# P and normalised x as fp16 planes turned by DMA, and scores, values and feed-forward of three query groups interleaved in 16 slots

## The reference

```python
def attn(x):                       # x already layer-normalised
    qkv = x[:, :, :64].fp16 @ w[:64].fp16 + x[:, :, 64:192] @ w[64:192] + x[:, :, 192:].fp16 @ w[192:].fp16
    q, k, v = split(qkv)
    s = softmax((q / sqrt(256)) @ k.T)
    return (s @ v) @ out_w.T + out_b

def ffn(x):                        # x already layer-normalised
    x_prev = x shifted by one token, zero ahead of the first
    r = sigmoid((mu_r * x + (1 - mu_r) * x_prev) @ W_r.T)
    k = relu((mu_k * x + (1 - mu_k) * x_prev) @ W_k.T) ** 2
    return r * (k @ W_v.T)

x = x + layernorm(attn(layernorm(x)))
x = x + layernorm(ffn(layernorm(x)))
```

## Time and profile before

| | |
|---|---|
| median of 3 runs | 1007.12 us (1006.1 to 1007.22) |
| span of the profiled execution, first to last instruction | 1005.9 us |
| PE busy | 969.4 us (96%) |
| DVE busy | 779.2 us (77%) |
| ACT busy | 555.6 us (55%) |
| POOL busy | 367.6 us (37%) |
| DMA queue of the kernel | 9.0% of 16 engines |
| mean granted TensorE clock | 0.991 of full |

### The profile page before, as it was taken

One profiled execution on the slowest core, in us unless ns is written; L12 is line 12 of the kernel. 1 busy time (PEld: TensorE's weight loads), 2 busy tenths in 40 slices (PEclk: granted clock), 3 DMA queues, 4 the chain that ended last, 5 costly groups with the idle time before them and its releaser, 6 DMA issues.

```text
span 1005.9 us, 16314 instructions
## 1 busy us (share of the span) xinstructions
PE 969.4 (96%) x5480; PEld 826.4 (82%) x5480; DVE 779.2 (77%) x1951; ACT 555.6 (55%) x936; POOL 367.6 (37%) x487
## 2 busy tenths in 40 slices
PE   5999999999999999999999999999999999999964
PEld 4788888888888888888888888888888888888953
DVE  5647678798877868888786867879887786877788
ACT  5744636475763736546674563647576463654533
POOL 2202434252542514434252342515344251443334
PEclk9999999999999999999999999999999999999987
DMA  6200000010100401010010400001000010101001
GB/s 183 65 20 22 1 22 22 1 43 1 42 2 14 113 3 43 1 42 2 1 43 1 126 1 24 23 1 43 1 31 13 0 43 1 43 1 34 10 1 42
DMA packets 44763, 28.28 MB, mean 28 GB/s; under 512 B 18432, under 2 KB 44416, under 8 KB 44672
## 3 DMA queue, kind: packets, MB, share of 16 engines
q1 hardware_dynamic: 44672, 27.14, 9.0%
HBM read 18.75 MB, written 8.39 MB: 27 GB/s over the span
## 4 chain that ended last, share of the span: by engine, by line
PE 92%; DVE 5%; ACT 1%; issue 1%; SPq 1%; DMA 0%; POOL 0%; POOLq 0%; DVEq 0%
PE S L1185 10%; PE S L1158 6%; PE S L1164 6%; PE S L1160 6%; PE S L1159 6%; PE S L1163 6%; PE M L1115 6%; PE M L1116 6%; PE M L1117 6%; PE Y L1314 6%; PE Y L1315 6%; PE Y L1319 6%; PE Y L1316 6%; PE Y L1318 5%; PE M L1206 1%; DVE att L819 1%
## 5 line engine op out<-in xcount | busy, mean ns | idle before, releaser
L728 DVE TENSOR_TENSOR pt_lo<-S,pt_hi 128x512 fp32r<-128x512 f32 x256 | 172.0, 676 | 114.7 <-ACT pt_hi L459 114.1
L774 DVE TENSOR_SCALAR_CACHE_REDUCE probs<-S 128x512 f32<-128x512 f32 x256 | 169.4, 682 | 72.4 <-PE S L1164 71.6
L459 ACT ACTIVATE pt_hi<-S 128x512 fp32r<-128x512 f32 x256 | 150.0, 596 | 80.2 <-PE S L1185 71.9
L504 ACT ACTIVATE probs<-probs,neg_max 128x2048 f32<-128x2048 f32 (+2 forms) x80 | 132.7, 1661 | 39.8 <-DVE scaled_max L778 39.8
L1185 PEld LDWEIGHTS S<-ident,probs 128*128 128x128 f32 x936 | 115.0, 141 | 27.5 <-DVE q_lo L728 0.4
L1185 PE MATMUL S<-ident,probs 128*128 128x128 f32 x936 | 135.9, 272 | 0.0
L1314 PE MATMUL Y<-pt_hi,v_hi 128*128 128x512 f32 x240 | 109.0, 454 | 0.3 <-ACT pt_hi L459 0.3
L837 DVE RECIPROCAL tmp<-tmp 128x256 f32<-128x256 f32 x60 | 104.6, 1743 | 0.0
L1158 PE MATMUL S<-xt_low,q_hi 128*128 128x512 f32 x256 | 102.2, 399 | 1.2 <-DVE wt_lo L728 0.5
L1164 PE MATMUL S<-xt_hi,q_lo 128*128 128x512 f32 x256 | 101.1, 395 | 0.0
L1160 PE MATMUL S<-xt_lo,q_hi 128*128 128x512 f32 x256 | 101.0, 395 | 0.0
(11 more groups left out here) (218 smaller groups left out, 2205.6 us busy)
## 6 DMA issues: line engine op xcount, KB each, us to landing
x_res<-in_L_attn_x SPq DMA_DIRECT2D x16, 512.0 KB, 3.3
out_x<-gate SPq DMA_DIRECT2D x15, 512.0 KB, 2.9
xin<-in_L_attn_x SPq DMA_DIRECT2D x32, 128.0 KB, 3.2
xin<-in_L_attn_x SPq DMA_DIRECT2D x16, 256.0 KB, 3.7
out_x<-gate SPq DMA_DIRECT2D x2, 256.0 KB, 2.1
probs<-in_L_attn_weight_qkv SPq DMA_DIRECT2D x3, 128.0 KB, 2.7
probs<-in_L_attn_weight_qkv SPq DMA_DIRECT2D x1, 256.0 KB, 3.0
tmp<-in_L_attn_out_w SPq DMA_DIRECT2D x1, 256.0 KB, 3.9
```

Of the source, the lines that this page charges most:

```text
L728: return dve.tensor_tensor(out_lo, psum, f32(hi), ALU.subtract)
L774: dve.tensor_scalar(probs[:, t, c * BLK:(c + 1) * BLK], S[u % 4][:, :], 1.0, None, ALU.mult, ALU.max, accum_out=chunk_max[:, t, c:c + 1]). ...
```

## The change

**What it does.** (1) Normalised x is scaled by 2^11 and written by ACT and DVE as three fp16 planes for each 128-token tile: columns 0 to 127, columns 128 to 255, and the remainder of the latter (`planes`). One DMA transpose for each 512-token block (`turn_planes`) makes `turned` from them. The planes serve as values, the turned planes as keys. (2) P is made as exp with a bias that scales it by 2^15, then split by ACT (`probs_high`) and DVE (`probs_low`) in two fp16 planes of 128x2048, and each plane is turned by one DMA transpose from SP (`turn_probs`): 8 a group, of 512 KB each. (3) The folded query-key weights and the queries become fp16 pairs too, scaled by a maximum found on the chip (`weight_scale`, `weight_factors`). (4) Scores and values are fp16 products: five of 512 columns for a unit as before, and five of 256 columns for each of 16 key tiles in each half of a group (`attend`), 160 in place of 80. (5) The stages are gone: in each of 16 slots of a step g, PE makes one score unit of group g and two key tiles of group g-1, and the projection, norms and feed-forward of group g-2 (its end reaches into g+1) lie in slots given by a table. There are 19 steps (`LAST`): the first has scores alone, the 17th has values but no scores, the last two only what follows. (6) Sigmoid is one ACT instruction; exp plus one and the reciprocals on DVE go. (7) The last group's work in halves goes. (8) Blocks of x are loaded to two buffers and prepared every tenth slot.

The core of the diff (setup of weights and unchanged feed-forward bodies left out):

```diff
+    PROJECT, ATTEND, NORM_ATT, RESIDUAL, RES_STATS, MIX_IN, TURN = 2, 3, 4, 5, 7, 8, 9
+    MIX, SPLIT_MIX, RECEPT, KEYS, SQUARE, VALUES, GATE, NORM_GATE, FINISH, STORE = 11, 12, 13, 14, 15, 17, 18, 19, 19, 21
+    QUERY = 6
+    LAST = 19
...
-        xt_low = sb("xt_low", [P, N], F32R)
-        xt_hi = sb("xt_hi", [P, N], F32R)
-        xt_lo = sb("xt_lo", [P, N], F32R)
-        v_hi = sb("v_hi", [P, NKT, D], F32R)
-        v_lo = sb("v_lo", [P, NKT, P], F32R)
+        planes = sb("planes", [P, 2, NKT, 3, P], F16)
+        turned = sb("turned", [P, 2, NKT, 3, P], F16)
...
+        probs = sb("probs", [P, 2, N])
+        p_hi = sb("p_hi", [P, 2, N], F16)
+        p_lo = sb("p_lo", [P, 2, N], F16)
+        pt_hi = sb("pt_hi", [P, 2, NKT, HALF], F16)
+        pt_lo = sb("pt_lo", [P, 2, NKT, HALF], F16)
...
+            def turn_planes(n):
+                b, i = divmod(n, NJ)
+                kts = slice(i * NT, (i + 1) * NT)
+                if b >= 2 and i == 0:
+                    sp.wait_ge(s_done, (b - 1) * NJ * UNITS)
+                sp.wait_ge(plane_lo_made, n + 1)
+                sp.dma_start_transpose(turned[:, b % 2, kts].rearrange("p k l t -> p (k l) t"),
+                                       planes[:, b % 2, kts].rearrange("p k l d -> p (k l d)")).then_inc(xt_in[i], 16)
+
+            def turn_probs(g, t):
+                a, cols = t // PT, slice((t % PT) * P, (t % PT + 1) * P)
+                if g >= 1:
+                    sp.wait_ge(pv_done, 2 * (g - 1) + a + 1)
+                sp.wait_ge(p_hi_made, g * NT + t + 1)
+                sp.dma_start_transpose(pt_hi[:, a, :, cols], p_hi[:, t % 2, :]).then_inc(pt_in[t], 16)
+                sp.wait_ge(p_lo_made, g * NT + t + 1)
+                sp.dma_start_transpose(pt_lo[:, a, :, cols], p_lo[:, t % 2, :]).then_inc(pt_in[t], 16)
...
+            for g in range(LAST):
+                for s in range(UNITS):
+                    if s == 1 and 1 <= g <= G:
+                        turn_probs(g - 1, 2)
+                    if s == 4 and 1 <= g <= G:
+                        turn_probs(g - 1, 3)
+                    if s == 8 and g < G:
+                        turn_probs(g, 0)
+                    if s == 11 and g < G:
+                        turn_probs(g, 1)
+                    if (n := prep(g, s, 6)) is not None:
+                        turn_planes(n)
+                    if (n := prep(g, s, -8)) is not None:
+                        reload_x(n)
+                    if (q := at(g, s, STORE)) is not None:
+                        store(q)
+                    if s == 9 and 1 <= g <= G:
+                        load_residual(g - 1)
...
+            def probs_high(g, t):
+                n = g * NT + t
+                act.wait_ge(exp_made, n + 1)
+                if n >= 2:
+                    act.wait_ge(pt_in[(t + 2) % NT], 32 * ((n - 2) // NT + 1))
+                copy(p_hi[:, t % 2, :], probs[:, t % 2, :]).then_inc(p_hi_made, 1)
...
+            def receptance(q):
+                for i in range(2):
+                    act.wait_ge(rec_done, q * 2 + i + 1)
+                    act.activation(rec[:, i, :], M[i][:, :], ACT.Sigmoid).then_inc(rec_made, 1)
...
+            def score_out(g, u):
+                t, c = unit(g, u)
+                n = g * UNITS + u
+                dve.wait_ge(s_done, n + 1)
+                if c == 0 and g * NT + t >= 2:
+                    dve.wait_ge(p_lo_made, g * NT + t - 1)
...
+            def probs_low(g, t):
+                dve.wait_ge(p_hi_made, g * NT + t + 1)
+                dve.tensor_tensor(p_lo[:, t % 2, :], probs[:, t % 2, :], p_hi[:, t % 2, :],
+                                  ALU.subtract).then_inc(p_lo_made, 1)
...
-            def turn_probs(g, kt):
-                if kt == 0:
-                    pe.wait_ge(exp_made, g * EXPS + NT)
-                if kt == NC:
-                    pe.wait_ge(exp_made, (g + 1) * EXPS)
-                for t in range(NT):
-                    mm = pe.transpose(T[kt % 4][:, t * P:(t + 1) * P], probs[:, t, kt * P:(kt + 1) * P], ident[:, :])
-                mm.then_inc(p_turned, 1)
...
+            def attend(g, a, kt):
+                b = g // NJ
+                if kt == 0:
+                    for t in range(a * PT, (a + 1) * PT):
+                        pe.wait_ge(pt_in[t], 32 * (g + 1))
...
+                pe.matmul(to[:, 0, :], low, p_h, start=first, stop=False, skip_group_check=True)
+                pe.matmul(to[:, 0, :], low, p_l, start=False, stop=final, skip_group_check=True)
+                pe.matmul(to[:, 1, :], high, p_h, start=False, stop=False, skip_group_check=True)
+                pe.matmul(to[:, 1, :], high, p_l, start=False, stop=False, skip_group_check=True)
+                mm = pe.matmul(to[:, 1, :], rest, p_h, start=False, stop=final, skip_group_check=True)
...
+            for g in range(LAST):
+                for s in range(UNITS):
+                    if g < G:
+                        scores(g, s)
+                    if 1 <= g <= G:
+                        attend(g - 1, s // 8, 2 * (s % 8))
+                        attend(g - 1, s // 8, 2 * (s % 8) + 1)
```

More of the change, by code:

```diff
@@ L122, in sandwich @@
         xm_lo = sb("xm_lo", [P, 2, HALVES, BLK], F32R)
-        yk_hi = sb("yk_hi", [P, HALVES, BLK], F32R)
-        yk_lo = sb("yk_lo", [P, HALVES, BLK], F32R)
+        rec = diff
         S = [bank(f"S{i}") for i in range(4)]
-        T = S[2:] + S[:2]
-        Y = [bank(f"Y{i}") for i in range(HALVES)]
+        Y = [bank(f"Y{i}") for i in range(2)]
         M = [bank(f"M{i}") for i in range(2)]
[L131 to L136, removed]
         def f32(ap):
@@ L537, in squares, with copy @@
[L537 to L549 removed]
+            def copy(out_, in_, scale=1.0):
+                return act.activation(out_, in_, ACT.Copy, scale=scale)
@@ L1133, in queries @@
-            def queries(j, banks):
-                tokens = bass.ds(j * BLK, BLK)
+            def queries(g):
+                b, j = divmod(g, NJ)
+                pe.wait_ge(xt_in[j], 16 * (b + 1))
+                kts = slice(j * NT, (j + 1) * NT)
+                low, high, rest = (turned[:, b % 2, kts, l, :] for l in range(3))
                 for m in range(HALVES):
                     cols = slice(m * P, (m + 1) * P)
-                    two(banks[m][:, :], wt_hi[:, QK, 0, cols], wt_lo[:, QK, 0, cols], xt_low[:, tokens], True, False)
-                    three(banks[m][:, :], wt_hi[:, QK, 1, cols], wt_lo[:, QK, 1, cols], xt_hi[:, tokens],
-                          xt_lo[:, tokens], False, True).then_inc(q_done, 1)
@@ new lines, in queries, with scores @@
+                    pe.matmul(to, qk_hi[:, 0, cols], low, start=True, stop=False)
+                    pe.matmul(to, qk_lo[:, 0, cols], low, start=False, stop=False)
+                    pe.matmul(to, qk_hi[:, 1, cols], high, start=False, stop=False)
+                    pe.matmul(to, qk_hi[:, 1, cols], rest, start=False, stop=False)
+                    pe.matmul(to, qk_lo[:, 1, cols], high, start=False, stop=True).then_inc(q_done, 1)
+            def scores(g, u):
+                t, c = unit(g, u)
+                n, b = g * UNITS + u, g // NJ
@@ new lines, in scores @@
+                if n >= 4:
+                    pe.wait_ge(s_copied, n - 3)
+                rows, kts = slice(t * P, (t + 1) * P), slice(c * NT, (c + 1) * NT)
+                low, high, rest = (turned[:, b % 2, kts, l, :] for l in range(3))
+                to = S[n % 4][:, :]
+                pe.matmul(to, q_hi[:, g % 2, 0, rows], low, start=True, stop=False)
+                pe.matmul(to, q_lo[:, g % 2, 0, rows], low, start=False, stop=False)
+                pe.matmul(to, q_hi[:, g % 2, 1, rows], high, start=False, stop=False)
```

1489 lines of the change are left out of this document (512 added, 977 removed).

## The result

The changed kernel takes 1093.44 us (median of 4 executions, 1088.53 to 1100.53) beside 1007.17 us for the kernel before. The ratio is 1.086, with a 95% interval of 1.082 to 1.090. The forecast was 891 us, faster. The profiled execution took 1090.8 us with a span of 1088.9.

What follows compares the result with a forecast made beforehand. PE's own work was taken to bound the kernel. 27 + 25 + 37 + 707 (14 steps of 49.5 + 1) + 37 + 57 gave 890 us of span, 891 measured; own range 854 to 953, for 8 in 10 up to 1130.

Steps and rivals of the forecast that it cites:

- PE's work: PE's products in one group: 49.5 us after the change, with 48.4 and 51.9 kept as ends; 59.93 before.
- The DMA term: Turned planes of P and x: 8.75 DMA transposes a group, 26 us of DMA in 50, beside PE.
- (b): DMA binds: PE waits for turned P in slots 0 and 8, T above 5.8 us, slower than before; chance 0.22.
- (c): DMA turns each plane 128x128 tile after tile with latency exposed, T 53 us, time 7 ms; chance 0.05.
- T: DMA engines' time for one transpose of 512 KB: taken as 3 us, between ends of 2.1 and 360.
- the sign given: In the profile after, a DMA transpose was to land in under 6 us.
- I charge 1 us of waits a step, and keep 0 and 3: PE's waits on late results in each steady step: 1 us, range 0 to 3, on top of 49.5.
- the 57 us a step: Stated sign of error: the prediction is wrong if a step exceeds 57 us for any reason.
- 15 of 19 us: Old group's chain from projection in slot 2 to the mixed input's turn in slot 9: needs 15 us of 19.
- the four score banks: PE runs four score banks ahead, three slots or 9 us, set against late results on other engines.
- rival (a): In-order waits: a late result each step, from POOL or DVE, costs 4 to 7 us; 933 to 975; chance 0.14.
- Start and tail: Outside the steady steps: 27 us to first scores, step 0 25, step 1 37, step 16 37, tail 57.

Runs made afterwards that it cites:

- the moves: Against the kernel after: DVE's gating ahead of the low plane, ACT's attention norm behind the high plane, ACT's sigmoid ahead of the high plane; 975.25 us, ratio 0.969.
- the fastest: DVE multiplies the gate ahead of slot 2's score unit, on top of the reordered tanh kernel with later chain and x blocks every 13th slot; 928.1 us, ratio 0.921.
- tanh: Sigmoid made as (1 + tanh(x/2))/2, on top of the kernel with three instruction moves; 967.71 us, ratio 0.961.
- spread out: Blocks of x prepared every 13th slot in place of every 10th, on top of the kernel with the old group's chain a slot later; 940.59 us, ratio 0.934.
- quarters: Each low plane of P made by DVE as four instructions of 512 columns, on top of the kernel with the old group's chain a slot later; 985.85 us, ratio 0.979.

## Why the prediction was wrong

**PE's work was right.** I took 49.5 us a group. Score products now stand 0.215 us apart and products of 256 columns 0.109 (timeline of the kernel after, the ends of a run of four intervals and of one of nine):

```profile
474.38 0.38 PE L806 MATMUL S<-turned,q_hi 128*128 128x512 f16 x1
...
475.24 0.38 PE L810 MATMUL S<-turned,q_lo 128*128 128x512 f16 x1
...
480.50 0.27 PE L825 MATMUL Y<-pt_hi,planes 128*128 128x256 f16 x1
...
481.48 0.27 PE L829 MATMUL Y<-pt_hi,planes 128*128 128x256 f16 x1
```

By the earlier trace rows they were 0.232 and 0.118. Scores 80 x 0.215 = 17.2, values 160 x 0.109 = 17.4, queries 2.2, the rest unchanged at 12.2: 49.0 us, near the good end of 48.4. The guess that most of the excess over 213 ns would go with fp16 fits. That reading 4-byte operands is its cause was not tested.

**The DMA term was right, and (b) and (c) fell.** T was put at 3 us. The queue's 41.6% of 16 engines is 7248 engine-us; less the traffic of before, 9.0% of its 16 x 1005.9 = 1448, and over 128 planes of P and 16 of x at three quarters, that is 2.6 us a plane, and the planes' packets come to some 20 ns each, as the 256- and 512-byte runs of the earlier trace rows had it at 22. Rival (b) needed 5.8. A transpose lands 3.8 to 4.0 us after its issue in the median, and never later than 5.9, where 6 was the sign given:

```profile
pt_hi<-p_hi SPq DMA_TRANSPOSE x64, 3.8
pt_lo<-p_lo SPq DMA_TRANSPOSE x64, 4.0
```

Of the Trainium skill's two figures, the 261 GB/s of DMA: Bandwidth & Descriptors, section on latency and other measured facts (by it T is an estimated 2.0 us), was the nearer. The 1309 ns a tile of VectorE: DVE Perf Modes, section on the three transpose paths, by which rival (c) had 2.9 ms, is not the rate here: 16 tiles of a plane cost 2.6 us.

**The step that failed** is "I charge 1 us of waits a step, and keep 0 and 3". The waits were 10.4 us a step, and PE's busy time was 4.4 us a step over the forecast, most of it slower clock behind the waits; that gives 64.3 by the window and 64.0 by the markers. It passed the 57 us a step beyond which the prediction called itself wrong. Three things went wrong in it.

First, it was priced from loads and not from queues. DVE at 80% and ACT at 73% of a 50 us step do leave room, and after the moves they fit: the same instructions ran at 55.3 us a step. But room says nothing about order. In the text I followed single results and asked only whether each had time in all ("15 of 19 us"); I did not set down, slot by slot, what stands ahead of each one on its engine. I named the low plane of 2.3 us, but behind the gating of slot 1, as the one that waits. It was the one that others wait behind, and so was ACT's high plane of 1.9.

Second, the slack I set against them was the four score banks. They cover a late evacuation of scores: PE waited for that 8.0 us in the whole kernel, all in step 0. They do not cover a product of the old group, which stands in PE's own order between score units. There one late bank stops everything.

Third, rival (a) had the mechanism, the places ("PE waits for DVE or POOL in slots 9 to 14") and even the table loads, but with a price of 4 to 7 us for one late result. There were four in each step, they add up, and the clock adds to them. The forecast with 13.5 us more in fourteen steps is 1080, close to what was measured. Its chance was 0.14; it should have been the forecast's equal. And for a case on the far side of 1007 I had looked to DMA alone.

**The clock** had no term at all. It stood at 0.62 behind a wait of 2.4 us and at 0.93 over four steps. Over the twelve steps between the markers PE's products were busy 643.4 us at 0.93 in the kernel after, and 603.0 us at 0.99 in the fastest, whose twelve steps take 619.2 us. So 40 of the 149 us between them, 3.4 a step, are busy time, the rest is idle time. No run changed the clock without changing the waits.

**Start and tail** were 19 and 17 us too short. The first scores came at 24.4 us, before the 27 I gave. Of the 19 us 9 are lost in step 0: first value product at 60.7 where I had 52, with the planes of the first tiles in series behind exp. The other 10 lie between it and the first marker, where the same waits of PE begin. The fastest kernel keeps 10 of the 19 and 12 of the 17: 12 x 1.1 + 10 + 12 is 35 of the 36 us by which its span of 926.1 stands over the forecast. So, once its order is right, the idea comes within 4% of the forecast, with tanh, which the forecast did not have, for 7.5 us of it.

**Open**: why a block of x still costs 2 us when spread out; the 12 us that the tail stays over its forecast; halves in the tail, as before, which were not tried.

## What to carry to other kernels

When work for a late group is woven by hand into fixed slots, don't price it from each engine's load: list for each product that the bound engine must not miss what stands ahead of its inputs on every queue in that slot, and put long instructions behind short ones that someone waits for. Longer instructions (one 2048-column plane for four of 512) save their overhead but make each place behind them four times as late. And where TensorE is granted a lower clock behind a wait, as here (0.62 behind 2.4 us), the wait costs more than its length.

## What was not expected of the hardware

- A DVE operation with two SBUF inputs holds POOL for its length: 0.20 us became 2.16, or 0.56 beside quarters; and POOL holds DVE, 2.50 us of quarters becoming 3.98.
- A switch between exp's and sigmoid's tables is a load of 1283 ns, twice a step, and tanh needs none.
- The 4 us behind a wait of 2.4 us ran at a granted clock of 0.62: products of 512 columns stood 0.43 us apart, then 0.23.
- A turned fp16 plane of 512 KB costs 2.6 us on all 16 DMA engines, some 20 ns a packet where the plain runs of 256 and 512 bytes before had 22. To issue one, SP is busy 1.6 us (high planes) or 1.8 (low planes) in the median, 1.3 to 3.8 in all.
